# Building the edge-count matrix of a graph network: item offsets loaded four groups at a time, start and softmax transfers arranged anew

## The chip, the cores and the metric

One core of a Trainium2 chip runs the whole program. The metric is the device time of one execution in microseconds (us). The engines have their own queues and run unsynchronised but for semaphores: TensorE (PE, with PEld for its weight loads), VectorE (DVE), ScalarE (ACT), GpSimd (POOL) and SyncE (SP, which here only issues transfers). A "q" behind a name (PEldq, ACTq) marks what an engine's sequencer does itself, such as loading registers.

## The reference

Four graph layers run one after another on 3125 nodes of 96 features and 100,000 edges, sorted by destination. The change lies in the stage ahead of them all, in which edges become a dense matrix of counts that later layers multiply by, and in which the edge softmax of layer 1 is computed.

```python
edge_index = jnp.stack([src, dst])
h = jnp.maximum(_layernorm(x, axis=-1), 0.0)
x = x + _L0_gnn_ref(h, qW, kW, vW, src, dst)              # attention over edges
...
# layer 1: softmax of the edge weights over the edges of one destination
seg_max = jax.ops.segment_max(edge_weights, tgt, num_segments=n)
e = jnp.exp(edge_weights - seg_max[tgt])
denom = jax.ops.segment_sum(e, tgt, num_segments=n)
gamma = e / denom[tgt]
...
# layer 2: plain sum over edges
h_e = jax.ops.segment_sum(h[src], dst, num_segments=h.shape[0])
```

## The kernel before

The program has stages that all engines enter together (`meet`). The first, `build_*`, fills `CT`, a matrix in SBUF of 25 x 3148 fp16 per partition: the count of edges from each source (128 partitions x 25) to each destination (columns).

**Items.** The sorted edges are cut into items of up to 128 edges whose destinations lie in a window of 4 columns. There are 1565 items, in 13 blocks (`NJ`) of 128 slots. Four items make a group `g`, two groups a set `s` of 198; 392 groups are present. Even groups come from the first half of the items, odd groups from the second.

**One group.** DVE makes, for a set, the one-hots `oneS` (source within 128) and `mov` (which of 25 x 4 cells), three sets deep (`DEEP`). PE runs four matmuls L486 (128x100, one per item, placed in PSUM at an offset from a register, relative to the first item's window), then L490, which adds what `CT` holds at the group's window (400 columns, start from a register). ACT copies the 400 columns back to `CT` (L521) and signals `placed`. L490 of group g waits for `placed` of g-2, and the first matmul for `placed` of g-4 (the PSUM bank).

**Registers.** The window offsets lie in `wI0` (block 0) and `wI` (blocks 1 to 12) in SBUF. `load_windows` (L424) loads them on PE (four values for a group) and ACT (one value), for group i+1 ahead of the work of group i. The load instruction is recorded under L429.

**Before the loop.** From the last destination of each of 782 chunks (`lw`), DVE derives `le`, and compares it with `iotaS` (made by POOL, L177) in seven comparisons `past` (L279). PE sums these over partitions: L439 for block 0, L443 for blocks 1 to 12 (84 matmuls). `slots` (DVE L289, L292) turns the sums into windows `win` and chunk numbers `cI`; POOL gathers the chunks' sources and destinations (`gather`, L192 and L195, two buffers), and makes from them the keys (L210 to L222) with `hi` of DVE (`high`, L402). PE turns the keys (`turn_items`, L454 and L456), ACT stores them in `KL` (`keep_items`, L506), and the one-hots of that block can be made. Meanwhile `CT` is zeroed in three parts: POOL columns 0 to 7000 (L189), DVE 7000 to 23000 (L298), ACT the rest to 39350 (L510). PE and ACT wait for all three parts before the loop.

**In the loop.** At set 16(j-1)+1 DVE makes `high(j)`, at 16(j-1)+6 PE turns block j. The edge softmax runs in 13 steps on DVE (`soft_step`, with small turns on PE), one behind each set 18 + 8k: step 0 writes two pads and signals `soft_pad`, for which SP waits (L236) ahead of six transfers (L237 to L242) of destinations and edge weights; step 1 waits for these, steps 1, 3, 6, 8 and 10 begin a scan along the edges (`scan_a`), steps 2, 4, 7, 9 and 11 carry it over partitions, and step 10 has a reciprocal of 782 columns. All of it is queued on DVE between the one-hots.

The memory of `past` and `iotaS` is used again by later buffers (`oneS`, `mov` and the softmax's arrays).

## Time and profile before

| | |
|---|---|
| median of three runs | 1519.89 us (1519.3 to 1521.41) |
| the profiled execution | 1519.76 us, span 1518.0 us |
| PE busy | 1238.1 us (82%) |
| DVE busy | 1019.6 us (67%) |
| ACT busy | 714.4 us (47%) |
| POOL busy | 540.8 us (36%) |

The `build_*` stage ends at about 484.7 us of the span; the rest belongs to the layers. A row of the timeline has the start, the duration, the engine, line and operation, then what is written and read, the shape, how many were merged, and in brackets how long the engine was idle before and what ended that. A group row has the count, the busy time and the mean ns of one, and behind it the idle time before and its releasers. A windows row has the stretch, its length, for each engine the busy time and number of instructions, then the granted clock of PE (1.00 is the upper level), the share of the DMA engines and GB/s. Ends of matmuls are modelled.

### The profile page before, as it was taken

To read this page: it belongs to the slowest core of one execution; us is meant where nothing else is said; L and a number is where in the kernel's file an instruction comes from. 1 tells how busy PE (TensorE), PEld (TensorE's weight loads), DVE (VectorE), ACT (ScalarE), POOL (GpSimd) and SP (SyncE) were. 2 spreads that over 40 slices of the span, in tenths; PEclk is the share of its full clock that TensorE was granted. 3 is DMA by queue.
4 is the path that set the end of the run, shared out by engine and by line. 5 is a ranking of instruction groups with operands and counts; after the bars stand their busy time and mean duration, and the time that the engine had idled before them with its cause. 6 is when DMAs were issued, how large, how long until landed. Compare 5 with 4: busy or idle time off the path is not lost.

```text
span 1518.0 us, 25052 instructions
## 1 busy us (share of the span) xinstructions
PE 1238.1 (82%) x8411; PEld 682.4 (45%) x8411; DVE 1019.6 (67%) x1866; ACT 714.4 (47%) x985; POOL 540.8 (36%) x322
## 2 busy tenths in 40 slices
PE   1867998799998994778877778778478799999994
PEld 0434454455554551212221222222168698778783
DVE  7637777766555443898999999888695653432276
ACT  3433454445454213997989899898410000001131
POOL 5311122212200006397999899897300000000000
PEclk9855555555555796898999999999779799999997
DMA  0010000000000341111111111111111100010111
GB/s 7 8 46 5 5 5 5 4 16 5 5 2 14 79 102 47 29 44 39 44 45 41 43 44 51 50 45 51 39 44 49 50 24 13 1 27 8 48 35 32
DMA packets 61190, 47.36 MB, mean 31 GB/s; under 512 B 31216, under 2 KB 59504, under 8 KB 60944
## 3 DMA queue, kind: packets, MB, share of 16 engines
q1 hardware_dynamic: 59440, 44.04, 10.3%
q0 software_dynamic: 1632, 1.72, 0.4%
q8 instruction: 77, 1.26, 0.3%
q14 instruction: 41, 0.34, 0.1%
HBM read 31.94 MB, written 13.79 MB: 30 GB/s over the span
## 4 chain that ended last, share of the span: by engine, by line
PE 55%; DVE 22%; ACT 12%; issue 4%; SPq 2%; DMA 1%; another core or an unknown queue 1%; POOL 1%; DVEq 0%; ACTq 0%
PE PS L1275 16%; PE PS L486 14%; DVE Eb L1081 12%; PE PS L490 8%; ACT Eb L1046 5%; ACT Eb L1048 5%; PE PS L1631 3%; PE PS L995 2%; PE PS L815 2%; PE PS L984 2%; PE PS L1266 1%; DVE Eb L1075 1%; SPq L241 1%; PE PS L799 1%
## 5 line engine op out<-in xcount | busy, mean ns | idle before, releaser
L922 POOL TENSOR_SCALAR Eb<-Eb 128x1024 f32<-128x1024 f32 (+4 forms) x164 | 404.5, 2481 | 69.8 <-ACT Eb L1050 69.4
L1081 DVE SCALAR_TENSOR_TENSOR Eb<-Eb,PS 128x1024 f32<-128x1024 f32 (+4 forms) x350 | 365.1, 1083 | 49.3 <-ACT Eb L1048 36.4
L521 ACT ACTIVATE CT<-PS 128x400 f32 x392 | 197.6, 504 | 238.1 <-PE PS L490 237.5
L486 PE MATMUL PS<-mov,oneS 128*128 128x100 f16 x1565 | 249.7, 257 | 45.2 <-DVE mov L394 36.2
L1275 PE MATMUL PS<-hs,CT 128*128 128x192 f16 (+3 forms) x2500 | 269.8, 271 | 6.2 <-DVE B L1476 2.7
L1050 ACT ACTIVATE Eb<-PS,small 128x1024 f32<-128x1024 f32 (+5 forms) x257 | 247.1, 995 | 34.3 <-PE PS L995 20.4
L486 PEld LDWEIGHTS PS<-mov,oneS 128*128 128x128 f16 x1565 | 162.7, 105 | 221.3 <-issue 141.5
L1275 PEld LDWEIGHTS PS<-hs,CT 128*128 128x128 f16 (+1 forms) x2500 | 233.1, 101 | 39.7 <-DVE B L1476 3.2
L394 DVE TENSOR_TENSOR oneS<-iotaX,KL 128x1024 f16<-128x1024 int16 x198 | 138.4, 699 | 139.5 <-PE PS L490 136.1
L995 PE MATMUL PS<-Qb,Kb 96*128 96x512 f16 (+3 forms) x700 | 199.6, 368 | 26.2 <-ACT Eb L1050 13.3
L490 PE MATMUL PS<-CT,identb 128*128 x392 | 197.2, 503 | 0.7 <-ACT CT L521 0.4
L1005 PE MATMUL PS<-Eb,V 128*25 128x512 f32 (+3 forms) x1400 | 173.3, 568 | 2.1 <-DVE Eb L1081 2.0
L984 PE MATMUL PS<-identb,CT 128*128 128x128 f16 (+1 forms) x625 | 69.3, 226 | 88.0 <-DVE Eb L1081 84.0
L995 PEld LDWEIGHTS PS<-Qb,Kb 96*128 96x128 f16 (+1 forms) x700 | 47.5, 100 | 160.3 <-ACT Eb L1050 84.4
L215 POOL TENSOR_SCALAR key<-hi 128x128 f32<-128x128 int32 x13 | 8.3, 636 | 311.0 <-DVE hi L402 311.0
L394 DVE TENSOR_TENSOR mov<-iotaM,KL 128x800 f16<-128x800 int16 x198 | 116.8, 590 | 0.0
L1046 ACT ACTIVATE Eb<-PS,small 128x1024 f32<-128x1024 f32 (+4 forms) x93 | 102.8, 1105 | 24.9 <-PE PS L995 14.5
L984 PEld LDWEIGHTS PS<-identb,CT 128*128 128x128 f16 (+1 forms) x625 | 39.9, 101 | 164.0 <-DVE Eb L1081 151.4
L1476 DVE TENSOR_REDUCE SG<-PS 128x96 f32<-128x288 f32 (+3 forms) x75 | 30.1, 420 | 104.0 <-PE PS L1275 103.6
L1048 ACT ACTIVATE Eb<-Eb,small 128x1024 f32<-128x1024 f32 (+4 forms) x93 | 97.6, 1050 | 3.0
L1369 ACT ACTIVATE hs<-PS 96x96 f32<-96x96 f32 x9 | 2.2, 248 | 180.4 <-PE PS L1296 180.4
L1075 DVE TENSOR_SCALAR Eb<-Eb 128x1024 f32<-128x1024 f32 (+4 forms) x93 | 66.5, 715 | 19.9 <-ACT Eb L1050 8.4
(262 smaller groups left out, 993.5 us busy)
## 6 DMA issues: line engine op xcount, KB each, us to landing
Kb<-kd SPq DMA_DIRECT2D x168, 96.0 KB
qd<-QH SPq DMA_DIRECT2D x24, 96.0 KB, 1.9
kd<-QH SPq DMA_DIRECT2D x24, 96.0 KB, 2.1
XG<-x_d SPq DMA_DIRECT2D x12, 192.0 KB, 2.4
x_d<-XG SPq DMA_DIRECT2D x12, 192.0 KB, 1.8
hs<-t_d SPq DMA_DIRECT2D x12, 192.0 KB, 2.5
Qb<-qd SPq DMA_DIRECT2D x4, 384.0 KB
CT<-x_d SPq DMA_DIRECT2D x1, 1200.0 KB, 7.5
```

Of the source, the lines that this page charges most:

```text
L394: return v.tensor_tensor(out.rearrange("p e (c two) -> p e c two", two=2), v_in, k_in, ALU.is_equal)
L486: t.matmul(to, K.oneS[:, s % DEEP, 4 * r + k, :], K.mov[:, s % DEEP, 4 * r + k, :].rearrange("p (a w) -> p a w", a=25), start=(k == 0), st ...
L490: t.matmul(ps, K.identb[:, :], K.CT[:, :, bass.ds(vals[0], 4 * W)], start=False, stop=True, skip_group_check=True).then_inc(S("counted"), 1)
L521: a.activation(K.CT[:, :, bass.ds(vals[0], 4 * W)], K.bank(g % 4)[:, 0:25 * 4 * W].rearrange("p (a c) -> p a c", a=25), ACT.Copy).then_inc ...
L922: g.tensor_scalar(e, e, ELO, None, ALU.max).then_inc(S("floored"), 1)
L995: m = p.matmul(bank(h)[0:r, 0:wb], K.Kb[:, it % NK, h, 0:r], K.Qb[:, b % 2, h, 0:wb], start=True, stop=True)
L1005: m = p.matmul(bank(4)[32 * h:32 * h + 25, 0:wb], K.V[0:r, t, h, :], K.Eb[0:r, (2 * it + h // 2) % NE_, h % 2, 0:wb], start=(t == 0), stop ...
L1046: a.activation(e, ps, ACT.Relu, bias=K.ten[0:r, 0:1], scale=K.unsc[0:r, :]).then_inc(S("score_read"), 1)
L1048: a.activation(e, e, ACT.Exp, bias=K.ten[0:r, 1:2]).then_inc(S("exp_a"), 1)
L1050: a.activation(e, ps, ACT.Exp, scale=K.unsc[0:r, :]).then_inc(S("score_read"), 1)
L1081: v.scalar_tensor_tensor(out=e, in0=e, scalar=EHI, in1=cn, op0=ALU.min, op1=ALU.mult).then_inc(S("weighed"), 1)
L1275: m = p.matmul(bank(t % FIRST)[0:r, 0:w], K.CT[:, a, 128 * t:128 * t + r], hs[:, a, :, :].rearrange("p k d -> p (k d)"), start=(a == 0), s ...
```

## The change

- `load_windows` loads for four groups at once: 16 values on PE and, with a stride of four, 4 values on ACT, at every fourth group, at the head of its own work and no longer one group ahead.
- Only block 0 is prepared before the loop: `iotaS` of 128 columns, `past` of 128 columns, `slots` and the windows of block 0. POOL makes the rest of `iotaS` behind `gather(0)`. DVE makes the other columns of `past` behind sets 0 to 3, PE sums blocks 1 to 12 behind sets 3, 4 and 5, DVE runs `slots` for them behind set 8, PE turns the windows behind set 8, DVE copies the table behind set 10. `high(1)` moves from set 1 to set 12, the turn of block 1 from set 6 to set 14; `gather(1)` comes after the first keys.
- The pads of the softmax are written behind set 8, so that its transfers can begin there; its steps 1 to 12 move six sets later (24 + 8k).
- Zeroing: POOL in three memsets (2000 before `gather(0)`, 3500 after it, 7000 after the keys of block 0), DVE 6500, ACT 15000 before `keep_items(0)` and 5350 after it. PE and ACT wait for all of them before the loop.
- `KL` is split (`KLa` for blocks 0 to 4, `KLb` for the rest), and `oneS`, `mov` and `cs` no longer share memory with `past`; `KLb` and the softmax's arrays now do.

```diff
-TURN_AT = {16 * (j - 1) + 6: j for j in range(1, NJ)}
-SOFT_AT = {18 + 8 * k: k for k in range(13)}
+TURN_AT = {14 if j == 1 else 16 * (j - 1) + 6: j for j in range(1, NJ)}
+HIGH_AT = {12 if j == 1 else 16 * (j - 1) + 1: j for j in range(1, NJ)}
+SOFT_AT = {24 + 8 * k: k for k in range(1, 13)}
+PAST_AT = {0: (0, 1), 1: (2, 3), 2: (4, 5), 3: (6,)}
+SUM_AT = {3: range(1, 5), 4: range(5, 9), 5: range(9, NJ)}
+SLOTS_AT, TABLE_AT = 8, 10
...
-ZG, ZV = 7000, 23000
+ZG1, ZG2, ZG3 = 2000, 5500, 12500
+ZV = ZG3 + 6500
+ZA = ZV + 15000
...
+    g.wait_ge(S("slot_w"), 1)
+    gather(0)
+    g.memset(K.CTf[:, ZG1:ZG2], 0.0).then_inc(S("zero_g"), 1)
+    g.iota(K.iotaS[:, 128:SLOTS], [[4, SLOTS // 8 - 16], [LH, 2], [1, 4]], base=4 * 16, channel_multiplier=0,
+           allow_small_or_imprecise_dtypes=True).then_inc(S("iota"), 1)
+    keys(0)
+    g.memset(K.CTf[:, ZG2:ZG3], 0.0).then_inc(S("zero_g"), 1)
+    g.wait_ge(S("slot_w"), 2)
+    gather(1)
...
     v.wait_ge(S("passed"), 1)
     slots(slice(0, 1), K.bank(5)[:, 0:1])
-    v.wait_ge(S("passed"), 2)
-    slots(slice(1, NJ), K.bank(4)[:, 0:NJ - 1])
-    v.memset(K.CTf[:, ZG:ZV], 0.0).then_inc(S("zero_v"), 1)
+    v.memset(K.CTf[:, ZG3:ZV], 0.0).then_inc(S("zero_v"), 1)
...
+        for t in PAST_AT.get(s, ()):
+            v.wait_ge(S("iota"), 7)
+            v.tensor_scalar(K.past[:, t, 128:SLOTS], K.iotaS[:, 128:SLOTS], K.le[:, t:t + 1], None, ALU.is_gt
+                            ).then_inc(S("past"), 1)
+        if s == SLOTS_AT:
+            v.wait_ge(S("passed"), 2)
+            slots(slice(1, NJ), K.bank(4)[:, 0:NJ - 1])
+            v.memset(prev[:, 0:1], -1).then_inc(S("soft_pad"), 1)
+            v.memset(dn[:, J - 1:J], 9000).then_inc(S("soft_pad"), 1)
+        if s == TABLE_AT:
+            v.wait_ge(S("windows"), 2)
+            v.tensor_copy(K.wI[:, :], K.bank(4)[0:NJ - 1, 128:256]).then_inc(S("reg_set"), 1)
...
-def load_windows(K, e, ety, g, n):
+def load_windows(K, e, ety, q, every):
-    j, o = g // 32, 4 * (g % 32)
-    row = K.wI0[0:1, o:o + n] if j == 0 else K.wI[j - 1:j, o:o + n]
+    j, o = q // 8, 16 * (q % 8)
+    row = K.wI0[0:1, o:o + 16:every] if j == 0 else K.wI[j - 1:j, o:o + 16:every]
...
-    vals = load_windows(K, t, mybir.EngineType.PE, 0, 4)
-    for i, g in enumerate(PRESENT):
-        if i + 1 < len(PRESENT):
-            nxt = load_windows(K, t, mybir.EngineType.PE, PRESENT[i + 1], 4)
+    for g in PRESENT:
         s, r = g // 2, g % 2
+        if g % 4 == 0:
+            quad = load_windows(K, t, mybir.EngineType.PE, g // 4, 1)
+        vals = quad[g % 4]
...
+            if s in SUM_AT:
+                m = later_sums(SUM_AT[s])
+                if NJ - 1 in SUM_AT[s]:
+                    m.then_inc(S("passed"), 1)
+            if s == SLOTS_AT:
+                t.wait_ge(S("slot_w"), 2)
+                t.matmul(bank(4)[0:NJ - 1, 128:256], K.win[:, 1:NJ], K.turnW[:, :], start=True, stop=True
+                         ).then_inc(S("windows"), 1)
...
-    a.activation(K.CTf[:, ZV:ZT], K.zf[:, 0:1].to_broadcast([128, ZT - ZV]), ACT.Copy).then_inc(S("zero_a"), 1)
+    a.activation(K.CTf[:, ZV:ZA], K.zf[:, 0:1].to_broadcast([128, ZA - ZV]), ACT.Copy).then_inc(S("zero_a"), 1)
     keep_items(0)
+    a.activation(K.CTf[:, ZA:ZT], K.zf[:, 0:1].to_broadcast([128, ZT - ZA]), ACT.Copy).then_inc(S("zero_a"), 1)
```

## Rows read from the trace of the kernel before

**Rows 1.** Windows: the CT loop, a stretch of it; PE, PEld, DVE, ACT, POOL busy, PEclk.
```profile
43.80:484.70 440.90, 396.31 (x1996) 209.47 (x1996) 280.39 (x469) 204.11 (x405) 87.57 (x105) 0.54 0.03 9
300.00:400.00 100.00, 97.52 (x489) 51.36 (x488) 61.00 (x105) 49.86 (x100) 21.78 (x27) 0.52 0.03 9
```

**Rows 2.** Windows of line L1275 alone, at the low clock: PE, PEld busy, PEclk.
```profile
1210.40:1215.60 5.20, 5.20 (x33) 4.91 (x33) 0.50 0.16 50
```

**Rows 3.** Timeline in the loop, PE's weight loads: start us, us.
```profile
51.82 0.47 PEld L486 LDWEIGHTS PS<-mov,oneS 128*128 128x128 f16 x4 [0.39 <-issue]
```

**Rows 4.** Line L429, the register loads: ns min/median/max, first and last start.
```profile
L429 PEldq TENSOR_LOAD <-wI x392: 326/331/772, 41.4 to 481.1; - x196
L429 ACTq TENSOR_LOAD <-wI x392: 273/279/470, 42.1 to 481.7; - x196
```

**Rows 5.** Groups by line and form, 44 to 486 us: L486.
```profile
L486 PE MATMUL PS<-mov,oneS 128*128 128x100 f16 x1565 | 249.7, 257 | 45.2 <-DVE mov L394 36.2 <-issue 3.5
```

**Rows 6.** Timeline around the softmax transfers: SP, DVE, PE.
```profile
78.32 0.36 SPq L237 DMA_DIRECT2D A<-in_dst  x1
...
114.75 0.97 DVE L347 TENSOR_TENSOR sp<-A 128x782 bf16<-128x782 int32 x1 [20.11 <-DMA wv<-in_edge_weight]
...
121.37 0.61 PE L486 MATMUL PS<-mov,oneS 128*128 128x100 f16 x4 [21.81 <-DVE mov L394]
```

**Rows 7.** Timeline at the loop's end, PE and ACT.
```profile
482.29 0.51 PE L490 MATMUL PS<-CT,identb 128*128 x1
...
482.92 0.50 ACT L521 ACTIVATE CT<-PS 128x400 f32 x1 [0.76 <-PE PS L490]
...
483.56 0.51 PE L490 MATMUL PS<-CT,identb 128*128 x1 [0.42 <-ACT CT L521]
```

**Rows 8.** Timeline of two softmax steps on DVE, and PE behind the second.
```profile
149.41 0.15 DVE L332 COPY cs<-PS 128x1 f32<-128x1 f32 x1
...
155.11 0.68 DVE L394 TENSOR_TENSOR oneS<-iotaX,KL 128x1024 f16<-128x1024 int16 x1
...
270.10 0.15 DVE L332 COPY cs<-PS 128x1 f32<-128x1 f32 x1
...
280.88 0.68 DVE L394 TENSOR_TENSOR oneS<-iotaX,KL 128x1024 f16<-128x1024 int16 x1
...
281.96 0.68 DVE L394 TENSOR_TENSOR oneS<-iotaX,KL 128x1024 f16<-128x1024 int16 x1
...
282.10 0.64 PE L486 MATMUL PS<-mov,oneS 128*128 128x100 f16 x4 [7.25 <-DVE mov L394]
```

**Rows 9.** The start: POOL and DVE in the timeline, past's line, L443, first L486.
```profile
1.19 5.67 POOL L177 IOTA iotaS<- 128x1664 int16 x1
...
8.94 6.36 POOL L189 MEMSET CT<- 128x7000 f32 x1
...
18.40 1.19 POOL L192 DMA_INDIRECT GS<-in_src,cI  x1 [3.11 <-DVE cI L292]
...
24.31 0.74 POOL L210 TENSOR_SCALAR dl<-GD,win 128x128 f32<-128x128 int32 x1
...
40.68 0.46 POOL L222 TENSOR_TENSOR va<-over,key 128x128 f32<-128x128 f32 x1
...
3.70 3.36 DVE L271 TENSOR_SCALAR lw<-lw 128x7 int32<-128x7 int32 x1
7.10 0.17 DVE L273 TENSOR_SCALAR le<-lw 128x7 f32<-128x7 int32 x1
...
25.08 13.39 DVE L298 MEMSET CT<- 128x16000 f32 x1 [3.28 <-issue]
...
L279 DVE TENSOR_SCALAR past<-iotaS,le x7: 634/643/6392, 7.5 to 16.8; 128x1664 f16<-128x1664 int16 x7
...
17.53 2.56 PE L443 MATMUL PS<-oneh,past 128*128 128x1 f16 x81
...
43.85 0.57 PE L486 MATMUL PS<-mov,oneS 128*128 128x100 f16 x4 [1.97 <-DVE mov L394]
```

More of the change, by code:

```diff
@@ L150, in alloc_build @@
     K.cc = sb(st, "cc", [128, 7], I32)
+    K.oneS = sb(st, "oneS", [128, DEEP, 8, 128], F16)
+    K.mov = sb(st, "mov", [128, DEEP, 8, 25 * W], F16)
+    K.cs = sb(st, "cs", [128, 4], F32)
     with ExitStack() as st2:
@@ L197, in gather, with keys @@
                              ).then_inc(S("gd_in%d" % (j % 2)), 16)
-    g.wait_ge(S("slot_w"), 1)
-    gather(0)
-    for j in range(NJ):
-        if j + 1 < NJ:
-            g.wait_ge(S("slot_w"), 2)
-            if j:
-                g.wait_ge(S("key"), j)
-                g.wait_ge(S("lo"), j)
-            gather(j + 1)
+    def keys(j):
         gd = K.GD[:, j % 2, :]
@@ L222, in build_gpsimd @@
         g.tensor_tensor(K.va[:, :], K.over[:, :], K.key[:, :], ALU.mult).then_inc(S("key"), 1)
+    g.wait_ge(S("slot_w"), 1)
[7 more added lines that the diff above has]
+    gather(1)
+    for j in range(1, NJ):
+        if j + 1 < NJ:
+            g.wait_ge(S("key"), j)
+            g.wait_ge(S("lo"), j)
+            gather(j + 1)
+        keys(j)
     g.wait_ge(S("key"), NJ)
@@ L278, in build_vector @@
     for t in range(7):
-        v.tensor_scalar(K.past[:, t, :], K.iotaS[:, :], K.le[:, t:t + 1], None, ALU.is_gt).then_inc(S("past"), 1)
+        v.tensor_scalar(K.past[:, t, 0:128], K.iotaS[:, 0:128], K.le[:, t:t + 1], None, ALU.is_gt).then_inc(S("past"), 1)
     v.wait_ge(S("identf"), 1)
@@ L336, in soft_step @@
     def soft_step(k):
-        if k == 0:
-            v.wait_ge(step, own.n)
-            v.memset(prev[:, 0:1], -1).then_inc(step, own.up())
-            v.wait_ge(step, own.n)
-            v.memset(dn[:, J - 1:J], 9000).then_inc(S("soft_pad"), 1)
-        elif k == 1:
+        if k == 1:
             v.wait_ge(S("dc_in"), 16)
@@ L440, in build_tensor, with later_sums @@
     m.then_inc(S("passed"), 1)
-    for j in range(1, NJ):
-        for t_ in range(7):
-            m = t.matmul(bank(4)[:, j - 1:j], K.past[:, t_, 128 * j:128 * j + 128], K.oneh[:, :], start=(t_ == 0), stop=(t_ == 6))
-    m.then_inc(S("passed"), 1)
     t.wait_ge(S("slot_w"), 1)
     t.matmul(bank(5)[0:1, 128:256], K.win[:, 0:1], K.turnW[:, :], start=True, stop=True).then_inc(S("windows"), 1)
-    t.wait_ge(S("slot_w"), 2)
-    t.matmul(bank(4)[0:NJ - 1, 128:256], K.win[:, 1:NJ], K.turnW[:, :], start=True, stop=True).then_inc(S("windows"), 1)
+    def later_sums(blocks):
+        t.wait_ge(S("past"), 14)
+        for j in blocks:
+            for t_ in range(7):
+                m = t.matmul(bank(4)[:, j - 1:j], K.past[:, t_, 128 * j:128 * j + 128], K.oneh[:, :],
+                             start=(t_ == 0), stop=(t_ == 6))
+        return m
     def turn_items(j):
@@ L496, in build_tensor @@
                 soft_step(SOFT_AT[s - 1])
-        vals = nxt
     t.wait_ge(S("counted"), len(PRESENT))
```

46 lines of the change are left out of this document (23 added, 23 removed).

## The prediction

> **What bounds the kernel now.** I read first the sum over the loop that builds CT, the only stage that the change touches (43.8 to 484.7 us): VectorE (DVE) is busy 280 of 441 us and ScalarE (ACT) 204, while TensorE (PE) shows 396, at a granted clock of 0.54, that is mostly 1.2 of 2.4 GHz [rows 1]. In a stretch without a stall PE starts 489 matmuls in 100 us; five make a group (four L486, one L490), so a group takes 1.02 us and a set (two groups) 2.04 us [rows 1]. Is that the array? At the low clock 33 matmuls of 192 columns fill 5.2 us, 158 ns each, or 0.82 ns a column [rows 2]; a group's 400 + 400 columns would need 0.66 us. So the array has 0.36 us to spare, and the timeline shows where: before the first weight load of each group PE sits 0.39 us on "issue", with nothing to wait for [rows 3]. The cause is in the list by line: before each group PE's sequencer runs one register load of 4 values, 331 ns in the median, 392 times; ACT runs one of 1 value, 279 ns [rows 4]. ACT's lies beside its own ACTIVATE (0.50 us of a 1.02 us group [rows 7]); PE's lies in the open. Sequencer work that is serial with matmul dispatch bounds the loop. Beside it stand stalls on DVE: PE idles 36.2 us on one-hots [rows 5], 21.8 of them once, after DVE waited 20.1 us for the softmax transfers [rows 6].
>
> Two near limits come up once the load is gone. Groups of the same parity are chained through CT (L490 reads what ACT placed two groups before): at the end of the loop the chain runs bare, 482.29, 482.92, 483.56, so 1.27 us per set [rows 7]. The array needs 1.33 us per set, DVE 1.08 (oneS to next oneS, 280.88 to 281.96) [rows 8].
>
> **Part 1, loads for four groups.** Per four groups PE drops three of four loads. One costs 0.331 us by its own duration and 0.39 by the idle [rows 3, 4]; I take 0.38, since the idle starts only after the weight load before it has ended, when the load is already under way. The load that stays fetches 16 values. Its price is not in the trace. Lower end: as now, 0.33. Upper end: in proportion, 4 x 0.331 = 1.32. The nearest rows are the two loads themselves: three more values cost 331 - 279 = 52 ns, 17 ns each (on two engines, but both sequencer work); twelve more cost 0.21, so 0.54. I take that. Four groups: 4 x 1.02 = 4.08, less 3 x 0.38, plus 0.21 = 3.15 us. Check against the limits: chain 2 x 1.27 = 2.54, array 2 x 1.33 = 2.66; both lie below 3.15, and the long load itself overlaps the L490 in the array, so neither binds for long. 98 fours: 98 x (4.08 - 3.15) = **-91 us**. ACT's load of 4 values (0.28 to 0.33) comes once in four groups, beside an ACTIVATE of 0.50: nothing. The load no longer comes a group ahead, but nothing that it waits for (reg_set) is late, and PE's sequencer runs it in order in either place.
>
> A rule speaks against this part. The Trainium skill (Runtime: NRT & Kernel Launch, Instruction fetch mechanics) says that a register load costs about 200 ns per register even in bulk, written of registers loaded from HBM. By it 16 values would take 3.2 us and four groups 5.8; here 4 values took 0.331 us, so the trace bears it out for SBUF in no way.
>
> **Part 2, softmax transfers begun early.** Now the pads are written at set 18 and the first transfer issues at 78.32; the last lands at 114.75, 36.4 us later [rows 6]. After the change the pads follow set 8 on DVE, when PE has ended set 5, some 12 us into the loop; issue to landing then ends some 49 us into it. DVE wants the data at set 32, when PE has ended set 29: 30 x 1.57 + 4 = 51 us. Just hidden, with 2 us of cover; uncovered it costs what is missing, up to some 10 us if the gathers of block 1 slow the same queues. What is late next are DVE's own steps. A step of 10.8 us (270.10 to 280.88) cost PE 7.25: a slack of 3.5 [rows 8]. The slack is three sets of one-hots held ahead, so it shrinks by 3 x (2.04 - 1.57) = 1.4, to 2.1. Steps: three of about 5.7 (149.41 to 155.11 is one) stall 3.6 each, the 10.8 one 8.7, two of about 3 some 0.9 each, refilling behind them 1 in all: 22. Now it is 36.2: **-14 us**.
>
> **Part 3, the start.** Now the first L486 is at 43.85 [rows 9]. What released it, backwards: keys on GpSimd (POOL) last at 40.68, waiting for hi, which stood behind DVE's memset of 13.39 us. Forward, as changed: iotaS of 128 columns in place of 1664 takes about 0.6 in place of 5.67 (so POOL is free for its memset at 3.9, not 8.94); lw is there at 3.70 [rows 9]; DVE's small steps behind it took 0.4 (from 7.10 to the first past at 7.5). The seven short past comparisons may be held by POOL's memset of 2000 (2000/7000 x 6.36 = 1.8, to 5.7), as one of the long ones was held (6.39 against a median of 0.64); they end near 6.7, and gather(0) issues near 7.6 in place of 18.40. Then on POOL: two gather issues 2.5 (the first was 1.19), memset of 3500 3.2, iota of 1536 columns 5.2, keys 4.2 (six steps between 0.46, as va, and 0.83, as dl with its gap), memset of 7000 6.4, which gates PE: 7.6 + 21.5 = 29.1, and the first load (0.5 to 0.8) 30. DVE's memset of 16000 now did not start until POOL's dl had ended, 3.28 us after it could have [rows 9]: the two seem to exclude one another. The new one of 6500 takes 6500/16000 x 13.39 = 5.4 and starts beside gather(0), so POOL may lose up to 5.4: 35.4. I take 33: **-11 us**, between -8 and -14. ACT's two pieces (15000 and 5350 columns, at DVE's 0.84 ns each 12.6 and, after its first keep_items, 4.5) are no later than POOL's.
> The Trainium skill (SBUF — State Buffer, SBUF: two separate sides) says that DVE and GpSimd hold a shared port pair for a whole instruction and that a DVE operation with two SBUF inputs contends only with a GpSimd one that reads; by it the past pieces wait for the last memset and the one-hots do not, and the start lies at the late end, 35.
>
> **Part 4, what moves into the loop.** The 84 later sums (81 in 2.56 us [rows 9]) now stand in PE's queue after sets 3 to 5: +2.7. The second windows matmul after set 8: +0.4. Seven past comparisons of 1536 columns on DVE, 0.6 each, two behind each of the first three sets: 1.2 + 1.08 against PE's 1.57 per set, so PE waits about +1.4. slots at set 8, the table copy at 10: small, within slack. gather(1) issues after slots; hi(1) at set 12 waits for it, keys(1) wait for hi, turn_items(1) at set 14 for keys, and one-hots of set 16 for keep_items: two sets of margin for the keys, and the turn only two sets ahead instead of ten: +0.5 (to +10 if the gather lands late behind the softmax transfers, which now issue at the same moment). Sum **+5 us**. Turns, softmax steps and highs of later blocks stay.
> The stages behind the loop are the same instructions: 0, give or take 3 for the clock that they meet.
>
> **Sum.** The profiled run took 1519.76 us (span 1518.0 and 1.8 around it), the median of three runs is 1519.89. 1519.8 - 91 - 14 - 11 + 5 = **1409 us**. The loop would last about 339 us in place of 440, from 33 to 372. DVE's 280 + 4 us fit into it.
>
> **Rivals.**
> 1. The load costs in proportion to its values (83 ns each): 1.32, four groups 3.93, set 1.96; loop saves 98 x 0.15 = 15, slack stays, softmax stalls 14: 1519.8 - 15 - 22 - 11 + 5 = 1477. For: 4 values is all the trace has. Against: the 1-value load is 0.28, so most of the price is fixed.
> 2. A limit behind it binds: array 1.33 per set and the load not overlapped, 2.66 + 0.60 = 3.26, or the keys of block 1 or the softmax transfers come 5 to 15 us late: 1420 to 1430. For: 2 us of cover only.
> 3. The load of 16 costs no more than that of 4, 0.33: four groups 2.94, 98 x 1.14 = 112, but DVE stalls grow by 3: 1391. Chain and array still fit.
> 4. The slower side: the 16 values are not fetched by one instruction but one by one, 16 x 0.33 (0.279 and the gap) = 5.4 per four groups: 2.56 + 5.4 = 7.9, +3.9 x 98 = 380, less 20: about 1880. It turns from gain to loss above some 1.9 us for all 16, about 120 ns a value. The present loads fetch four at once in 392 instructions for 392 groups, which speaks against it. The 200 ns a register of the Trainium skill (Runtime: NRT & Kernel Launch, Instruction fetch mechanics) would land on this side too, at an estimated 5.8 per four groups: 98 x 1.7 - 20, about 1665; the same row speaks against it.
> 5. It doesn't do what it says: the 16 are split into four loads of 4, each 0.38: four groups 4.08 as now, and 36 to 38 us gained by the rest: 1483. It shares the chance of rival 1.
>
> **How the numbers follow.** Forecast 1409, its own bounds 1398 to 1420: 0.62. Rival 1 with 5: 0.10. Rival 2: 0.15. Rival 3: 0.09. Rival 4: 0.02. No case for "same": 0.01, and 0.01 elsewhere. 1388 to 1440 takes in the forecast and rivals 2 and 3 and leaves out 1, 4 and 5. A measurement of this kernel tells about 0.2% (3 us) from no change. Faster 0.97, same 0.01, slower 0.02.
>
> **What would show it.** Register loads on PE: 99 or so, of 0.54 us. Three groups of four with no "issue" idle ahead of the first weight load, L490 to L490 about 0.64, the fourth about 1.2. PE's wait on one-hots near 24 us, no wait of DVE on the transfer of edge_weight, or below 5. First L486 at 30 to 36, the last near 372. DVE busier than 7 tenths of the loop. The prediction is wrong if the load of 16 takes over 0.8 us, if L490 waits for ACT in most groups, or if PE stands at set 14 or 16.

## The result, and the profile after

| | before | changed |
|---|---|---|
| median, us | 1520.65 (1519.3 to 1522.18) | 1454.76 (1452.33 to 1457.21) |
| ratio to before | | 0.9566 [0.9547, 0.9586] |
| profiled execution, us | 1519.76 | 1454.33 |
| its span, us | 1518.0 | 1452.3 |

The change gains 65.9 us; 111 were forecast, so 45 are missing, and the time lies 15 us above the range. Where is the missing part? The page of the changed kernel gives the busy time of each engine:

```profile
PE 1142.7 (79%) x8411; PEld 676.2 (47%) x8411; DVE 1008.8 (69%) x1873; ACT 717.7 (49%) x986; POOL 538.7 (37%) x325
```

Only the CT loop and what lies ahead of it were touched, so the sum over windows is the next view (columns as in [rows 1]; lines of the changed kernel stand lower in the file: L516 is the old L486, L520 the old L490, L559 the old L521, L455 the old L429, L408 the old L394):

```profile
29.10:417.10 388.00, 299.91 (x2082) 205.62 (x2082) 281.99 (x480) 203.69 (x405) 85.52 (x109) 0.68 0.03 11
```

The loop lasts 388.0 us against 440.9 [rows 1]. Three pieces add up to the whole: it starts at 29.10 instead of 43.85 [rows 9], 14.75 us earlier; it is 52.9 us shorter; and from its end to the end of the span lie 1035.2 us (1452.3 - 417.1) against 1033.3 (1518.0 - 484.7), 1.9 more. 14.75 + 52.9 - 1.9 = 65.7, the difference of the spans. The forecast had 101 us for the loop, so the loop is where it failed. DVE and ACT did the same work in it (282.0 and 203.7 us against 280.4 and 204.1), and the gap is on PE's side.

The clock column needs care. The trace has no clock record before 50.5 us (58.7 us in the kernel before), and the row counts that time as 1.00, though L520 takes 0.53 us there, as at the low level. Counted as low, the loop's mean is 0.65 in place of 0.68, and 0.52 in place of the 0.54 of [rows 1].

The register loads by their line (ns min/median/max, first and last start; compare [rows 4]):

```profile
L455 ACTq TENSOR_LOAD <-wI x99: 884/907/1209, 27.7 to 413.4; - x99
L455 PEldq TENSOR_LOAD <-wI x99: 1101/1107/1512, 27.7 to 412.7; - x99
```

There are 99, as meant, but one takes 1.107 us on PE where the sum had 0.54, and 0.907 on ACT where it had at most 0.33. How the loop looks with them, in the timeline of PE (start us, us, idle before):

```profile
182.44 0.61 PE L516 MATMUL PS<-mov,oneS 128*128 128x100 f16 x4 [0.73 <-ACT CT L559]
182.92 0.51 PE L520 MATMUL PS<-CT,identb 128*128 x1
...
183.57 0.54 PE L520 MATMUL PS<-CT,identb 128*128 x1
...
184.23 0.54 PE L520 MATMUL PS<-CT,identb 128*128 x1
...
184.90 0.54 PE L520 MATMUL PS<-CT,identb 128*128 x1
186.19 0.61 PE L516 MATMUL PS<-mov,oneS 128*128 128x100 f16 x4 [0.75 <-ACT CT L559]
186.65 0.51 PE L520 MATMUL PS<-CT,identb 128*128 x1
```

Read the starts of L520. Three steps of 0.65, 0.66 and 0.67 us follow one another (182.92, 183.57, 184.23, 184.90): the "issue" idle of every group [rows 3] is gone there, and a group takes the 0.66 us that the prediction gave the array at 1.2 GHz. The fourth step takes 1.75 us (184.90 to 186.65): 0.66 and nearly the whole load (1.107) on top. Over all fours of the loop the median from an L520 to the fourth one behind it is 3.77 us; before it was 4.15 for the L490. The sum had 3.15. Put the measured load into its own formula, 3.15 - 0.54 + 1.11 = 3.72, and it is nearly what was found.

Is the array the limit in the three short steps? The trace has stretches at both levels, and the duration of L520 tells which: 0.51 to 0.54 us at the low level, 0.34 at the high one. At the high level the steps are hardly shorter. First three L520 of the changed kernel, then two L490 of the kernel before:

```profile
286.88 0.34 PE L520 MATMUL PS<-CT,identb 128*128 x1
...
287.52 0.34 PE L520 MATMUL PS<-CT,identb 128*128 x1
...
288.17 0.34 PE L520 MATMUL PS<-CT,identb 128*128 x1
```

```profile
162.91 0.34 PE L490 MATMUL PS<-CT,identb 128*128 x1
...
163.93 0.34 PE L490 MATMUL PS<-CT,identb 128*128 x1
```

Over the loop of the changed kernel a step without a load is 0.67 us in the median at the low level and 0.65 at the high one. In the kernel before a step is 1.02 at both, which is the plainest sign that the loop before was not bound by the array. What stands beside the array at 0.65 is again PE's sequencer: it runs one FUSED_REGOPS (37 to 51 ns, register arithmetic on an offset) ahead of each L516 but the first of a group and ahead of each L520, and at the high level the weight loads behind them start 0.12 us apart (287.266 and 287.390).

The waits of the loop show a trap (us in total, times, longest):

```profile
PE PS L516 <- ACT CT L559: 70.9, 94, 1.0
...
PE PS L516 <- DVE mov L408: 15.1, 7, 7.2
```

The first line looks as if ACT now held PE up, 0.75 us at each fourth group. The experiments below show that it does not. The second line is the stalls on one-hots: 15.1 us against 36.2 [rows 5].

### The profile page after: what moved, and what is told of

It is laid out like the page before. It is cut to its first block, busy times and chain, and to the rows that moved or that the text cites. A ratio compares the mean times of both kernels' runs of the same rounds, so it can differ in the third digit from the quotient of the medians.

```text
span 1452.3 us, 24477 instructions
## 1 busy us (share of the span) xinstructions
PE 1142.7 (79%) x8411; PEld 676.2 (47%) x8411; DVE 1008.8 (69%) x1873; ACT 717.7 (49%) x986; POOL 538.7 (37%) x325
## 3 DMA queue, kind: packets, MB, share of 16 engines
q1 hardware_dynamic: 59440, 44.04, 10.8%
## 4 chain that ended last, share of the span: by engine, by line
PE 52%; DVE 23%; ACT 15%; issue 6%; POOL 2%; another core or an unknown queue 1%; DMA 0%; ACTq 0%; SPq 0%; DVEq 0%
PE PS L1312 16%; DVE Eb L1118 12%; PE PS L516 10%; PE PS L520 8%; ACT Eb L1083 5%; ACT Eb L1085 5%; ACT CT L559 3%; PE PS L1032 3%; PE PS L1668 3%; PE PS L852 2%; PE PS L1021 2%; PE PS L1042 1%; PE PS L836 1%; POOL Eb L959 1%; DVE Eb L1112 1%
## 5 line engine op out<-in xcount | busy, mean ns | idle before, releaser
L959 POOL TENSOR_SCALAR Eb<-Eb 128x1024 f32<-128x1024 f32 (+4 forms) x164 | 405.1, 2484 | 71.6 <-ACT Eb L1087 71.2
L516 PE MATMUL PS<-mov,oneS 128*128 128x100 f16 x1565 | 220.1, 257 | 93.2 <-ACT CT L559 70.9
L559 ACT ACTIVATE CT<-PS 128x400 f32 x392 | 197.6, 504 | 185.7 <-PE PS L520 176.4
L516 PEld LDWEIGHTS PS<-mov,oneS 128*128 128x128 f16 x1565 | 160.4, 115 | 176.5 <-DVE mov L408 109.0
L520 PE MATMUL PS<-CT,identb 128*128 x392 | 182.6, 466 | 0.9 <-ACT CT L559 0.8
L408 DVE TENSOR_TENSOR oneS<-iotaX,KLb 128x1024 f16<-128x1024 int16 x118 | 82.7, 701 | 66.4 <-PE PS L520 65.4
L408 DVE TENSOR_TENSOR oneS<-iotaX,KLa 128x1024 f16<-128x1024 int16 x80 | 56.6, 708 | 38.0 <-PE PS L520 28.9
```

Of the source, the lines that this page charges most:

```text
L516: t.matmul(to, K.oneS[:, s % DEEP, 4 * r + k, :], K.mov[:, s % DEEP, 4 * r + k, :].rearrange("p (a w) -> p a w", a=25), start=(k == 0), st ...
L520: t.matmul(ps, K.identb[:, :], K.CT[:, :, bass.ds(vals[0], 4 * W)], start=False, stop=True, skip_group_check=True).then_inc(S("counted"), 1)
L559: a.activation(K.CT[:, :, bass.ds(vals[0], 4 * W)], K.bank(g % 4)[:, 0:25 * 4 * W].rearrange("p (a c) -> p a c", a=25), ACT.Copy).then_inc ...
L959: g.tensor_scalar(e, e, ELO, None, ALU.max).then_inc(S("floored"), 1)
```

## The experiments

All experiments start from the changed kernel. Chips differ in speed: the kernel before took 1502.3 us beside the first four, 1519.9 beside the next three, 1521.7 and 1521.4 beside the last five. So kernels are compared by their ratio to the kernel before on the same chip; 0.001 is 1.5 us.

The theory: batching puts one load in the place of four of one read each, but the one still pays for four reads, and PE's sequencer pays them in the open. The rivals: ACT, whose load grew too and runs in the same place, holds PE up; or the loads are cheap and a limit behind them binds (chain, array, one-hots).

**small_loads: the old loads in the changed kernel.** Everything else of the change stays.

```diff
-        if g % 4 == 0:
-            quad = load_windows(K, t, mybir.EngineType.PE, g // 4, 1)
-        vals = quad[g % 4]
+        vals = load_group(K, t, mybir.EngineType.PE, g, 4)
...
-            quad = load_windows(K, a, mybir.EngineType.Activation, g // 4, 4)
+        vals = load_group(K, a, mybir.EngineType.Activation, g, 1)
```

> The changed kernel, but PE loads 4 values and ACT 1 value for every group again. Theory (a load pays for each 16 bytes that it reads, about 0.21 us, and PE's dispatch stands still for its whole length): PE's load back at 0.33 us, four groups from 3.75 to about 4.08 us, 98 x 0.33 = 32 us slower than the changed kernel, about 1487 us; what stays of the gain, 34 us, is the start and the softmax transfers. Rival (ACT's load of 0.91 us holds PE up): without it four groups would be shorter than 3.75, and the kernel faster than 1455.

Measured: 1466.61 us, ratio 0.977 [0.9733, 0.9808]. The loads by their line:

```profile
L468 ACTq TENSOR_LOAD <-wI x392: 273/279/577, 27.5 to 447.4; - x196
L468 PEldq TENSOR_LOAD <-wI x392: 325/331/552, 27.5 to 446.7; - x196
```

The loads are back at 331 and 279 ns, four groups take 4.13 us, and the last matmul that adds `CT` (L529 here) starts at 447.99 in place of 415.76. So the big loads are worth 0.977 - 0.9566 = 0.020 or 31 us (32.2 in the loop's end), and start and softmax together 0.023 or 35 us. The second half of the change came out better than its share of the forecast (14 + 11 - 5 = 20 us); the first came out at a third of it.

**act_contig: ACT's four values side by side.** A second table holds only the window starts, so ACT reads four neighbouring int32 instead of every fourth one of sixteen. PE's load is left alone.

```diff
     v.tensor_copy(K.wI0[:, :], K.bank(5)[0:1, 128:256]).then_inc(S("reg_set"), 1)
+    v.tensor_copy(K.wA0[:, :], K.bank(5)[0:1, 128:256:4]).then_inc(S("reg_set"), 1)
...
-            quad = load_windows(K, a, mybir.EngineType.Activation, g // 4, 4)
+            quad = load_first(K, a, mybir.EngineType.Activation, g // 4)
```

> The changed kernel, but the first offsets of the groups also lie in a table of their own, so that ACT loads its four values from 16 neighbouring bytes instead of with a stride. Theory (price per 16 bytes read): ACT's load falls from 0.91 to about 0.33 us; the time stays within 3 us of the changed kernel, since PE's own load of 1.11 us covers it. Rival 1 (ACT's load holds PE up, 70.9 us of waiting in the profile): up to 70 us faster, about 1385. Rival 2 (price per value, 65 ns each, or 209 for ACT whatever the addresses): ACT's load stays at 0.47 to 0.91.

Measured: 1435.4 us, ratio 0.955 [0.9522, 0.9577].

```profile
L459 PEldq TENSOR_LOAD <-wI x99: 1101/1107/1386, 27.7 to 412.0; - x99
L472 ACTq TENSOR_LOAD <-wA x99: 304/309/627, 27.6 to 412.6; - x99
...
PE PS L531 <- ACT CT L574: 71.6, 94, 1.0
```

ACT's load fell from 907 to 309 ns, and nothing else moved: four groups stay at 3.76 us, and the line that blames ACT still says 71.6 us. So that wait is no wait on ACT. PE's sequencer is inside its load; ACT's ACTIVATE was merely the last semaphore event ahead of the matmul. The rival falls, as long as PE's own load stands in the same place (eight_groups below shows what happens where it doesn't). The run also gives the first hint at how a load is priced: four int32 that stand together cost 30 ns more than one (309 against 279), four that don't cost 628 ns more.

**no_loads: no register load after the first four groups.** The offsets of these are used again and again, so this kernel leaves out all later loads on PE and ACT, and its windows are the wrong ones. It leaves out more than that: with offsets that never change, most of the register arithmetic is gone from PE too (and from ACT). The rows of that line, first of this kernel, then of the changed one:

```profile
L516 PEldq FUSED_REGOPS  x12: 37/46/51, 29.1 to 31.1; - x12
```

```profile
L516 PEldq FUSED_REGOPS  x1173: 37/46/51, 29.1 to 414.9; - x196
```

With those of L520 it is 16 in place of 1565. So this run is a bound for a loop without any register work, and its gain is not the price of the loads alone.

```diff
-        if g % 4 == 0:
+        if g == 0:
             quad = load_windows(K, t, mybir.EngineType.PE, g // 4, 1)
```

> The changed kernel without register loads in the loop: PE and ACT load once and use the offsets of the first four groups for all, so that the wrong columns of CT are filled. Theory (serial loads are the bound, behind them the chain through CT of 2.54 and the array of 2.66 us per four groups): four groups 2.6 to 2.8 us, about 98 x 1.0 less, plus some 10 us of longer stalls behind VectorE's softmax steps: 1360 to 1375 us. If the chain or the array bound earlier than thought: above 1400.

Measured: 1334.64 us (one run), ratio 0.888. That is 0.068 or 104 us below the changed kernel; expected were 80 to 95.

```profile
29.20:315.50 286.30, 199.25 (x2082) 128.95 (x2081) 275.21 (x476) 184.96 (x404) 89.97 (x108) 0.88 0.04 14
...
PE PS L516 <- DVE mov L408: 83.1, 123, 11.0
```

The loop is now 286.3 us, and DVE is busy in 275.2 of them: with the register work gone the one-hots are the bound, and PE waits 83.1 us for them. Four groups take 2.35 us in the median, against 2 x 1.08 = 2.16 for two sets on DVE [rows 8]. Neither chain (2.54) nor array (2.66) binds as the prediction had them: the granted clock is 0.88 in this loop (0.68 in the changed one), and a group that need not wait for DVE takes 0.35 us at the high level, so both limits, read at the low clock, give way. The clock alone doesn't do it: at the same high level the changed kernel's steps stay at 0.65. The change of clock is seen in the timeline of PE:

```profile
203.45 0.52 PE L516 MATMUL PS<-mov,oneS 128*128 128x100 f16 x4 [10.98 <-DVE mov L408]
...
207.19 0.54 PE L516 MATMUL PS<-mov,oneS 128*128 128x100 f16 x4
...
207.85 0.34 PE L516 MATMUL PS<-mov,oneS 128*128 128x100 f16 x4
```

Behind an idle of 10.98 us four matmuls take 0.52 to 0.54 us; from 207.85, after unbroken work, 0.34. Four groups went from 3.77 to 2.35, 1.42 us for a load of 1.11. The 0.31 beyond it comes from the other groups, where the higher clock and the missing register arithmetic act together; this run doesn't part them, and without the second, 0.65 a group is the least that the changed kernel shows. What the median gains DVE takes away again in its long steps (the 10.98 us above is one, 7.17 in the changed kernel), so that over the loop 102 us remain of 98 x 1.42 = 139.

**late_pads: the softmax transfers late again.** The pads are written behind set 18, as before the change, the steps stay where the change put them.

```diff
             slots(slice(1, NJ), K.bank(4)[:, 0:NJ - 1])
+        if s == 18:
             v.memset(prev[:, 0:1], -1).then_inc(S("soft_pad"), 1)
```

> The changed kernel, but the softmax pads, and with them the transfers, come behind set 18 as before, while the steps stay at sets 32 on. Theory: the pads come at about 62 us of the span in place of 42, the data land at 98, ten us after VectorE wants them at 88; 8 to 10 us slower than the changed kernel, about 1464. Rival (hidden anyway, or the transfer is faster alone): same time.

Measured: 1446.76 us, ratio 0.9618 [0.9582, 0.9653], which is 0.005 or 8 us above the changed kernel. The intervals just touch, but act_contig on the same chip is 11.4 us faster (1435.4), and in the profiled run the last matmul of the loop is 12.5 us later (428.28 against 415.76). DVE in the timeline, and PE's wait on one-hots:

```profile
101.00 0.97 DVE L361 TENSOR_TENSOR sp<-A 128x782 bf16<-128x782 int32 x1 [12.94 <-DMA wv<-in_edge_weight]
...
PE PS L517 <- DVE mov L408: 29.8, 8, 14.8
```

DVE waits 12.94 us for `wv`, and PE's wait on one-hots is back from 15.1 to 29.8. So this part of the change does what the prediction said: it takes the wait on the transfer away.

**changed_again and int16_table.** The changed kernel once more on another chip, and beside it the same kernel with the two tables in int16: 16 values in 32 bytes in place of 64. Is the price one per byte (then the load gets cheaper) or one per value?

```diff
-    K.wI0 = sb(st, "wI0", [1, 128], I32)
-    K.wI = sb(st, "wI", [NJ - 1, 128], I32)
+    K.wI0 = sb(st, "wI0", [1, 128], I16)
+    K.wI = sb(st, "wI", [NJ - 1, 128], I16)
```

> The changed kernel itself, beside the next two, as their measure: about 0.957 of the kernel before.

> The changed kernel, but the tables of offsets hold int16, so that PE's 16 values lie in 32 bytes in place of 64. Theory (about 0.07 us, 0.22 for each 16 bytes read, 0.01 for each value): PE's load falls from 1.11 to 0.07 + 2 x 0.22 + 0.16 = 0.67 us; four groups from 3.76 to 3.32, 98 x 0.44 = 43 us less, some 5 given back in stalls behind the softmax steps: 0.957 - 0.026 = 0.931 of the kernel before. Rival (each read fetches four values whatever their size, or the price is per value): the load stays near 1.11 and the time the same.

Measured: changed_again 1451.94 us, ratio 0.9558 [0.9529, 0.9587]. int16_table 1706.09 us, ratio 1.1224 [1.1191, 1.1258], and this is a miss by far:

```profile
L455 ACTq TENSOR_LOAD <-wI x99: 880/903/1080, 27.6 to 664.8; - x99
L455 PEldq TENSOR_LOAD <-wI x99: 3783/3787/3971, 27.7 to 664.2; - x99
```

Half the bytes take 3.4 times as long. 3.787 us for 16 values is 0.24 each, and ACT's four strided values cost the same in int16 (903) as in int32 (907). So neither bytes nor values alone count. The durations fit a price per read, some 0.2 us, where values are read one by one unless they are four int32 that stand together. A "read" is inferred here from the durations; no row of the trace shows one.

**act_shift: the same four neighbours, one int32 further on.** Is it enough that the values are neighbours, or must the four stand in one aligned block of 16 bytes? act_contig again, with the table shifted by 4 bytes, so that each four spans two blocks.

```diff
-    v.tensor_copy(K.wA0[:, :], K.bank(5)[0:1, 128:256:4]).then_inc(S("reg_set"), 1)
+    v.tensor_copy(K.wA0[:, 1:33], K.bank(5)[0:1, 128:256:4]).then_inc(S("reg_set"), 1)
...
-    j, o = q // 8, 4 * (q % 8)
+    j, o = q // 8, 4 * (q % 8) + 1
```

> As act_contig, but ACT's table of first offsets begins one int32 later, so that its four neighbouring values straddle two blocks of 16 bytes. If a load fetches aligned blocks: two reads, about 0.51 us. If it fetches up to four neighbouring int32 wherever they lie: 0.31 as before. The time of the kernel is the same in both.

Measured: 1452.96 us (one run, beside 1521.65; ratio 0.955).

```profile
L472 ACTq TENSOR_LOAD <-wA x99: 900/917/1265, 27.6 to 413.5; - x99
```

917 ns: as slow as strided. Two reads would have been about 0.5. Across a block's edge all four cost as if read singly.

All loads seen fit one rule, which stands on these seven medians: about 0.07 us, 0.2 per read (0.22 on PE), some 0.01 per value; four int32 in one aligned block of 16 bytes are one read, else each value is one.

| values | where | reads | engine | ns |
|---|---|---|---|---|
| 1 | int32 | 1 | ACT | 279 |
| 4 | one block | 1 | ACT | 309 |
| 4 | one block | 1 | PE | 331 |
| 4 | every fourth int32 | 4 | ACT | 907 |
| 4 | neighbours over a block's edge | 4 | ACT | 917 |
| 16 | four blocks | 4 | PE | 1107 |
| 16 | int16 | 16 | PE | 3787 |

**packed_both: all offsets of four groups in one read.** A group's four offsets fit into 18 bits (the first below 4096, the other three multiples of 4 up to 12), so DVE packs them into one int32, and one load of 4 values brings what four groups need. The price: registers must be taken apart, 28 more register instructions on PE in four groups.

```diff
+    return [[(x & 4095).with_bounds(min_val=0, max_val=NP - W)]
+            + [((x >> (8 + 2 * k)) & 12).with_bounds(min_val=0, max_val=3 * W) for k in range(1, n)] for x in vals]
...
-            quad = load_windows(K, t, mybir.EngineType.PE, g // 4, 1)
+            quad = load_packed(K, t, mybir.EngineType.PE, g // 4, 4)
```

> The changed kernel, but the four offsets of a group are packed into one int32 (12 bits and three of 2 bits), so that one load of 4 values (16 bytes) serves four groups on PE and on ACT; PE unpacks with register arithmetic, 28 more register instructions for four groups. Theory: the load falls to 0.33 us on PE and 0.31 on ACT, 0.78 less; but dispatch is serial, so each register instruction counts too, at 37 to 50 ns of its own as the address instructions now cost: 28 x 0.045 = 1.3 more; four groups 4.2 to 4.3 us, slower than the changed kernel by 45 us or more. Rival (register instructions hide behind the array): four groups 3.0, 70 us faster.

Measured: 1632.83 us (one run, beside 1519.92; ratio 1.074). A miss in size: four groups were to take 4.2 to 4.3 us, and take 5.75.

```profile
L487 PEldq TENSOR_LOAD <-wP x99: 327/332/520, 27.7 to 592.3; - x99
...
201.70 1.22 PE L547 MATMUL PS<-mov,oneS 128*128 128x100 f16 x4
...
L551 PE MATMUL PS<-CT,identb x392: 510/512/534, 29.5 to 595.4; 128*128 x196
```

The load is 332 ns, one read, as the rule says. But the four matmuls of a group now take 1.05 to 1.22 us in place of 0.54. The clock column seems to say that this happened with an array twice as fast:

```profile
200.00:300.00 100.00, 90.11 (x358) 37.63 (x357) 54.52 (x90) 36.94 (x73) 13.48 (x18) 1.00 0.01 4
```

It doesn't. The trace has no clock record before 622.9 us, behind this loop, so the 1.00 is an empty column. The row of L551 above, which adds `CT`, tells the level: all its 392 matmuls take 0.510 to 0.534 us, the low level, where the high one gives 0.34. The array is no faster than before; even so it isn't the bound, since 0.66 us a group would do.

The trace of PE's sequencer shows what is: between two weight loads stand two ALU_OPs and one FUSED_REGOPS, 36, 36 and 46 ns long, but starting at 205.666, 205.762 and 205.859. Each takes 0.096 us of the sequencer, not the 0.036 of its row, and the expectation had taken the row's. The 28 more at 0.096 are 2.7 us, the smaller load gives back 0.78: 3.77 + 2.7 - 0.78 = 5.7, and measured are 5.75. So the sequencer is the bound in both ways of getting the offsets, and a register instruction in the open costs nearly a third of a load of four values (0.096 against 0.331).

**eight_groups: 32 values at once, on PE alone.** If only the fixed part is saved by a bigger load, twice the size saves the 0.07 once more in eight groups, and nothing is lost, or so I thought.

```diff
-        if g % 4 == 0:
-            quad = load_windows(K, t, mybir.EngineType.PE, g // 4, 1)
-        vals = quad[g % 4]
+        if g % 8 == 0:
+            eight = load_eight(K, t, mybir.EngineType.PE, g // 8)
+        vals = eight[g % 8]
```

> The changed kernel, but PE loads 32 values for eight groups at once. Theory (0.07 us fixed, 0.22 for four neighbouring int32, 0.01 for each value): the load takes 0.07 + 8 x 0.22 + 0.32 = 2.15 us in place of two of 1.11, and one gap of 0.06 goes: 0.13 less in eight groups, 49 x 0.13 = 6 us, 0.952 of the kernel before in place of 0.956. If the price rose with the length of the load: slower.

Measured: 1469.5 us, ratio 0.9647 [0.9614, 0.968], 13 us slower than the changed kernel on that scale, not faster.

```profile
L468 PEldq TENSOR_LOAD <-wI x50: 2127/2132/2632, 27.7 to 426.1; - x50
...
L455 ACTq TENSOR_LOAD <-wI x99: 885/907/1073, 27.7 to 426.7; - x99
...
PE PS L528 <- DVE mov L408: 93.7, 43, 7.8
...
300.50 0.90 ACT L571 ACTIVATE CT<-PS 128x400 f32 x2 [0.55 <-PE PS L532]
...
300.08 0.34 PE L532 MATMUL PS<-CT,identb 128*128 x1
...
301.14 0.34 PE L532 MATMUL PS<-CT,identb 128*128 x1 [0.34 <-ACT CT L571]
```

The load costs what the rule gives (0.07 + 8 x 0.22 + 0.32 = 2.15; measured 2.13). Eight groups take 7.8 us in the median against 7.56, and 49 x 0.26 is the loss of 13 us. The row on one-hots looks like its cause (43 waits in place of 7), but it is the trap of the line on ACT again: 39 of the 43, 81.9 us, stand right behind a load of PE, and DVE itself is idle for up to 2.5 us there, waiting for PE. The other four come to 11.8 us, against 15.1 in the changed kernel.

The loss stands elsewhere. Only PE's load was made bigger; ACT still loads at every fourth group, 0.907 us, and at every second of these PE now has no load that covers it. ACT's load of 299.471 ends at 300.378, the ACTIVATE behind it runs from 300.50 to 301.01, and L532, which needs what this one placed, starts at 301.14, 1.06 us after the one before it in place of 0.65. That step of each eight groups is 1.02 us in the median, 0.67 in the changed kernel: 0.35 x 49 = 17 us, of which the saving on PE's side gives some back. So the run speaks against leaving ACT's load in the open, not against a bigger load on PE. The bigger load together with act_contig's table, where ACT's load is 309 ns, was not run.

**split_step: the long softmax step in three.** In the changed kernel the wait of 7.2 us in the line on L408 above is one step, seen in the timelines of DVE and PE:

```profile
232.31 5.04 DVE L395 RECIPROCAL A<-A 128x782 f32<-128x782 f32 x1
...
241.02 0.68 DVE L408 TENSOR_TENSOR oneS<-iotaX,KLb 128x1024 f16<-128x1024 int16 x1
...
242.24 0.61 PE L516 MATMUL PS<-mov,oneS 128*128 128x100 f16 x4 [7.17 <-DVE mov L408]
```

The step is cut at sets 107 and 110, with the next step at 115 in place of 112.

```diff
-            v.reciprocal(A1[:, :], A2[:, :]).then_inc(step, own.up())
+            v.reciprocal(A1[:, 0:H], A2[:, 0:H]).then_inc(step, own.up())
+        elif k == 13:
+            v.reciprocal(A1[:, H:J], A2[:, H:J]).then_inc(step, own.up())
             v.wait_ge(step, own.n)
             v.tensor_tensor(A3[:, :], wv[:, :], A1[:, :], ALU.mult).then_inc(step, own.up())
+        elif k == 14:
```

> The changed kernel, but softmax step 10 (10.8 us on VectorE in one piece, behind which PE stood 7.3 us) is cut into three, behind sets 104, 107 and 110 (half of the reciprocal; the other half and the product; the scan), step 11 comes at 115. Theory (a step stalls PE only by what it exceeds a slack of about 3 to 4 us): the pieces of 4.4, 3.5 and 2.9 us stall it by 1 at most; 6 to 7 us less, 0.952. If VectorE's work as a whole were the bound: the same time.

> Both of the above. Theory: they add up, 12 us less than the changed kernel, 0.948 of the kernel before.

Measured: split_step 1446.93 us, ratio 0.952 [0.948, 0.9561], 0.0046 or 7 us below the changed kernel (the intervals overlap; the loop of the profiled run is 4.9 us shorter, 382.3 against 387.2 from the first matmul to the end of the last); eight_split, which is both edits, 1460.84, ratio 0.9595 [0.9564, 0.9627]. The stall of 7.17 us became four of 0.5 to 1.3:

```profile
236.46 0.56 PE L521 MATMUL PS<-mov,oneS 128*128 128x100 f16 x4 [0.89 <-DVE mov L413]
...
238.86 0.62 PE L521 MATMUL PS<-mov,oneS 128*128 128x100 f16 x4 [0.95 <-DVE mov L413]
...
243.24 0.54 PE L521 MATMUL PS<-mov,oneS 128*128 128x100 f16 x4 [1.34 <-DVE mov L413]
...
249.11 0.61 PE L521 MATMUL PS<-mov,oneS 128*128 128x100 f16 x4 [0.48 <-DVE mov L413]
```

eight_split gains as much over eight_groups (8 us) as split_step over the changed kernel, but carries the loss by ACT's open load with it; its expectation rested on the one for eight_groups and fell with it.

**all_split: the other long steps in two as well.** Steps 1, 3 and 8 (5.7 us each) are cut ahead of their scans, at sets 35, 51 and 91.

```diff
-SOFT_AT.update({107: 13, 110: 14, 115: 11, 120: 12})
+SOFT_AT.update({107: 13, 110: 14, 115: 11, 120: 12, 35: 21, 51: 23, 91: 28})
...
+        elif k == 21:
             scan_a(A1, wv, ALU.add, ALU.max, -BIG, False)
```

> As split_step, and the three softmax steps of 5.7 us (1, 3 and 8, which cost the four groups around them 2.2 to 2.5 us each in the changed kernel) are cut in two as well, the scan three sets later. Theory (each piece of up to 3.5 us disappears in the three sets of one-hots held ahead): up to 2 us less for each, 4 to 6 us less than split_step, 0.948 to 0.949 of the kernel before. Rival (those 2.2 us are PE's own turns and lost rhythm, not the wait): the same as split_step, 0.952.

Measured: 1441.18 us, ratio 0.9469 [0.9438, 0.95].

```profile
29.20:405.20 376.00, 295.58 (x2082) 203.29 (x2081) 281.79 (x477) 202.66 (x404) 87.61 (x108) 0.70 0.04 11
```

The loop lasts 376 us, 12 less than the changed one's 388. PE's waits on one-hots (L524 in this kernel) fall to 7.9 us from 15.1. This is the fastest version by its ratio, 0.0097 or 15 us below the changed kernel (0.0089 or 13.5 us below changed_again), and with the same work on every engine: it only stands in smaller pieces. The rival (the same as split_step) falls: the loop is 5.8 us shorter than there. What it has left is the loads: its four groups still take 3.76 us.

## Why the prediction was wrong

The direction was right, the time (1454.8) lies above the range (1388 to 1440). Step by step:

- **The load of 16 values: the step that failed.** "Three more values cost 331 - 279 = 52 ns, 17 ns each ... twelve more cost 0.21, so 0.54." Measured 1.107 us. The rows used [rows 4] could not show the price: both loads, that of 1 and that of 4 values, are one read, so their difference holds the price of a value in a block already read (0.01 us and the difference of two engines) and none of a further read. 0.57 us times 98 is 56 us, more than the whole of what is missing. The part's bounds, 0.33 and 1.32, did hold the true value; I took a value in the lowest quarter as if it were known and gave the upper end a tenth of the chance. With the bounds in the range (1477 at its end) the range would have held. That the load might take "over 0.8 us" was named as what would make the prediction wrong.
- **Four groups, 4.08 to 3.15.** Measured 4.15 to 3.77: -37 us (98 x 0.38) for -91. The rest of the working held in its numbers: three groups at 0.66, the fourth with the load in the open. Its reason for the 0.66, the array at the low level, is half of the truth: where the clock is high the groups still take 0.65, and that the two limits lie so close is luck. By the rule of the table the saving is 3 x (0.33 + 0.06) less (1.107 - 0.331), or 0.39 per four groups: the fixed part of three loads and the gap around them, since the reads themselves are as many as before.
- **ACT's load: "beside an ACTIVATE of 0.50: nothing".** Its cost was put at 0.28 to 0.33; it is 0.907, since its values stand four apart. That this costs nothing all the same in the changed kernel is shown by act_contig, and that it does where PE's load doesn't cover it by eight_groups.
- **Softmax transfers and stalls, -14.** Measured 36.2 to 15.1, -21. No wait on the transfers: the first issues at 42.58, the data's first user starts at 88.24 without idle. The prediction's 2 us of cover was never tried, for with slower groups set 32 came later than it had; late_pads shows that the late transfers cost 8 to 13 us. The steps stalled less than expected (7.17 for the 10.8 us step, 8.7 expected) presumably for the same reason: the loads that cost PE its time give DVE its slack.
- **The start, -11.** Measured -14.75 (43.85 to 29.10), a little outside the -8 to -14 given. See its rows below.
- **What moves into the loop, +5.** Not measured by itself. The loop's 52.9 less 37 and 21 leaves +5. PE does not stand at set 14 or 16.
- **The stages behind, 0 give or take 3.** +1.9.

The forecast's error in one line: +54 on the loads, -4 on the start, -7 on the stalls, +2 behind, 45 together.

Of the rivals, the first (a price in proportion to the values) was the nearest in its mechanism, at 1.32 us a load and 1477; the load came to 1.107, which is a price in proportion to blocks of 16 bytes. Rival 4, a read for each value, is what int16_table ran into: it gave 3.8 us a load and a kernel 12% slower than before, on the side where the prediction put it ("above some 1.9 us for all 16"; its own terms, 4.08 - 3 x 0.38 - 0.33 + x against 4.08 + 0.2, put the turn nearer 1.7). The 200 ns a register of the Trainium skill (Runtime: NRT & Kernel Launch, Instruction fetch mechanics), which the prediction set aside for SBUF, is written of registers loaded from HBM; by these runs it is about the price of a read from SBUF as well: 3787 ns for 16 int16 values, 907 for 4 strided ones. What makes it look wrong in [rows 4] is that four int32 in one aligned block go together.

The start of the changed kernel, in the timeline (start us, us):

```profile
7.48 1.19 POOL L207 DMA_INDIRECT GS<-in_src,cI  x1 [2.67 <-DVE cI L315]
8.49 5.47 DVE L319 MEMSET CT<- 128x6500 f32 x1 [1.30 <-issue]
...
9.91 3.03 POOL L233 MEMSET CT<- 128x3500 f32 x1
...
21.50 5.93 POOL L237 MEMSET CT<- 128x7000 f32 x1
...
24.14 4.23 DVE L433 TENSOR_SCALAR past<-iotaS,le 128x1536 f16<-128x1536 int16 x2
...
29.10 0.60 PE L516 MATMUL PS<-mov,oneS 128*128 128x100 f16 x4 [6.79 <-issue]
```

The working forward held: gather(0) at 7.48 (7.6 expected), POOL's last memset from 21.50 to 27.43 with PE behind it. Two reasons made it 3.9 us better than the 33 taken. DVE's memset and POOL's ran beside each other (8.49 to 13.96 and 9.91 to 12.94, each at about its own price, 5.47 for 5.4 and 3.03 for 3.2), so the exclusion that I had read out of [rows 9] and put up to 5.4 us on does not hold for two memsets. And the parts of POOL came out a little shorter each. With no loss at all the prediction's own sum was 30. The comparison that POOL's last memset did hold (24.14) stands behind the one-hots of set 0, so it didn't hold the first matmul, and the late end of 35 never came.

## What to carry to other kernels

Interpolate the price of a bigger instruction only between rows that differ in the quantity that will grow; two rows that both lie within one unit (here one block of 16 bytes) show nothing of the next unit, and then the bounds are the forecast. Register loads from SBUF are paid by the read: keep the values as int32, four together and aligned, take out of a batch only the fixed part as gain, and don't buy fewer reads with register arithmetic. Where an engine runs ahead by a few buffers, long steps are best cut small: all_split gained 13 to 15 us by this alone. A cost that is hidden is hidden only as long as what covers it: ACT's load was free beside PE's, and eight_groups lost 13 us when PE's was moved from its side. To tell the array from the sequencer, compare the same step at both levels of the clock, and take the level from the duration of a matmul, not from the clock column alone.

## What the runs showed of the hardware

- A register load costs about 0.2 us per read and 0.07 once. Four int32 in an aligned block of 16 bytes cost one read (309 to 331 ns); strided, over an edge, or as int16 every value costs one (907, 917 and 3787 ns).
- Register arithmetic on PE's sequencer is 36 to 46 ns long in its rows and takes 96 ns of time each (205.666, 205.762, 205.859), and it stands in the way of the matmuls behind it.
- A step of one group without a load is 0.67 us at the low level of the clock and 0.65 at the high one in the changed kernel; with its load it is 1.02 at both in the kernel before; and it is 0.35 at the high level in no_loads, where the register arithmetic is gone. So at the high level it is PE's sequencer and not the array that keeps a group at 0.65. Why the higher level is granted in one kernel and not in another is not settled by these runs: they changed it by the way, and none was made for it.
- Ahead of the trace's first clock record the clock column reads 1.00, while the durations are those of the low level: 0.53 us for L520 before 50.5 us in the changed kernel, 0.51 for L551 in all of the loop of packed_both.
- A memset of DVE and one of POOL ran side by side without loss. A comparison of DVE that came under POOL's memset took 3.71 us, until that had ended, and the one behind it 0.60; the two are the 4.23 above (1.13 for the next two, at 29.37). The Trainium skill (SBUF — State Buffer, SBUF: two separate sides) has DVE and GpSimd lock a shared port pair for a whole instruction where the DVE one is in a 2-port mode, or has two SBUF inputs and the GpSimd one reads. The trace agrees for the comparison as far as the hold goes, if it ran in such a mode, which no row shows; and a memset, which reads nothing, was not held.
- The idle time of an engine is put down to the last semaphore event: 71 us "on ACT" were a register load of the engine itself, and stayed at 71.6 when ACT's part was cut to a third.
